# A delta-rule attention block on one core: the order of the q/k/v products, what GpSimd convolves, and where squares and a square root stand

## The reference, cut to what matters

```
q = silu(short_conv(x @ Wq + bq, q_conv)); q = q / (norm(q per head) + 1e-6)
k = silu(short_conv(x @ Wk + bk, k_conv)); k = k / (norm(k per head) + 1e-6)
v = silu(short_conv(x @ Wv + bv, v_conv))
alpha = sigmoid(x @ Wa + ba); beta = sigmoid(x @ Wb + bb)
out_gate = silu(x @ Wg + bg)
```

## Time and profile before

| | us |
|---|---|
| median of 3 runs | 3601.69 |
| lowest, highest | 3601.07, 3607.35 |
| the profiled execution | 3599.55 |
| its span | 3597.8 |

### The profile page before, as it was taken

One profiled execution on the slowest core, in us unless ns is written; L12 is line 12 of the kernel. 1 busy time (PEld: TensorE's weight loads), 2 busy tenths in 40 slices (PEclk: granted clock), 3 DMA queues, 4 the chain that ended last, 5 costly groups with the idle time before them and its releaser, 6 DMA issues. The chain is left out here.

```text
span 3597.8 us, 192259 instructions
## 1 busy us (share of the span) xinstructions
PE 3307.7 (92%) x83216; PEld 2763.9 (77%) x83216; DVE 2783.0 (77%) x4457; ACT 1577.3 (44%) x2330; POOL 1840.8 (51%) x1713
## 2 busy tenths in 40 slices
PE   6999997799999999995999999999996986999999
PEld 4888886576767676775999999999996774888887
DVE  6767675787878787875888888888887866676765
ACT  3545543577777777671111111111113332545454
POOL 2232322556566565554777777777775431323232
PEclk9999999899999999997999999999998997999999
DMA  2222213132323232326676666666664773212121
GB/s 97 90 93 82 105 70 113 53 102 80 97 84 97 84 97 77 93 73 158 187 187 187 187 188 187 187 189 187 188 187 142 224 236 112 105 70 105 70 105 59
DMA packets 485370, 452.79 MB, mean 126 GB/s; under 512 B 55360, under 2 KB 448704, under 8 KB 465600
## 3 DMA queue, kind: packets, MB, share of 16 engines
q1 hardware_dynamic: 483008, 449.56, 41.3%
q10 hardware_dynamic: 2304, 2.49, 0.3%
HBM read 331.33 MB, written 120.60 MB: 126 GB/s over the span
## 5 line engine op out<-in xcount | busy, mean ns | idle before, releaser
L274 POOL TENSOR_TENSOR ffn_out<-ffn_gate,ffn_xres 128x512 f32<-128x512 f32 x128 | 173.3, 1382 | 790.3 <-DVE ffn_gate L235 789.9
L660 DVE SCALAR_TENSOR_TENSOR ain_conv<-ain_padded,ain_taps,ain_conv 128x512 f32<-128x512 f32 x384 | 416.5, 1085 | 13.6
L1320 ACT ACTIVATE rec_yf<-rec_ps_f 128x256 f32<-128x256 f32 x128 | 49.1, 384 | 632.2 <-DVE rec_f_t L1229 632.2
L761 POOL TENSOR_TENSOR ain_conv<-ain_conv,ain_term 128x512 f32<-128x512 f32 x192 | 272.3, 1418 | 16.0
L1101 POOL TENSOR_TENSOR rec_d_norm<-rec_dmat,rec_early 128x512 f32<-128x512 f32 x128 | 162.8, 1272 | 197.1 <-DVE rec_dmat L1179 197.1
L46 PE MATMUL ffn_ring<-ffn_mixrh,ffn_wrh 128*128 128x512 f32 x512 | 214.7, 419 | 20.4 <-DVE ffn_mixrl L180 20.4
L816 ACT ACTIVATE ain_buf<-ain_conv 128x512 f32<-128x512 f32 x192 | 121.0, 630 | 232.6 <-POOL ain_conv L761 147.1
L46 PE MATMUL ffn_ring<-ffn_mixkh,ffn_wkh 128*128 128x512 f32 x512 | 216.4, 423 | 0.0
L1376 PE MATMUL rec_ps_scores<-rec_qk_pe,rec_kb 32*32 32x64 f32 x8192 | 141.9, 217 | 70.3 <-issue 46.0
L46 PE MATMUL ffn_ring<-ffn_mixrh,ffn_wrl 128*128 128x512 f32 x512 | 201.9, 394 | 0.0
L46 PE MATMUL ffn_ring<-ffn_act_h,ffn_wvh 128*128 128x512 f32 x512 | 201.9, 394 | 0.0
(11 more groups left out here) (234 smaller groups left out, 10279.3 us busy)
## 6 DMA issues: line engine op xcount, KB each, us to landing
rec_early<-coeffs SPq DMA_DIRECT2D x512, 128.0 KB, 3.0
streams<-ain_buf SPq DMA_DIRECT2D x48, 1024.0 KB, 5.1
rec_qkv<-streams SPq DMA_DIRECT2D x126, 384.0 KB, 3.3
rec_qk_pe<-streams SPq DMA_DIRECT2D x127, 256.0 KB, 3.1
rec_late<-coeffs SPq DMA_DIRECT2D x504, 64.0 KB, 2.0
ffn_x<-in_x SPq DMA_DIRECT2D x16, 1024.0 KB, 8.4
ffn_xres<-in_x SPq DMA_DIRECT2D x16, 1024.0 KB
x<-ffn_out SPq DMA_DIRECT2D x16, 1024.0 KB, 4.6
```

What stands on the lines that cost most here:

```text
L274: last = nc.gpsimd.tensor_tensor(out[:, m, :], gate[:, m, :], xres[:, m, :], ALU.add)
L660: nc.vector.scalar_tensor_tensor(out=out[:], in0=pad[:, n:n + TOK], scalar=taps[:, u // KT, u % KT, n:n + 1], in1=out[:], op0=ALU.mult, op ...
L761: nc.gpsimd.tensor_tensor(out[:], out[:], term[:], ALU.add).then_inc(pool_conv, 1)
L1320: nc.scalar.activation(yf[:, 1], ps_f[:, :, 1, :], ACT.Copy).then_inc(f2_ready, 1)
```

## The change

The units are dealt out anew: u % 3 = 2 is v (unit 2 is v 0, 5 is v 1, 8 is v 2, 11 is v 3), the others are q 0 to 3 and k 0 to 3 in order. So the products run q q v q q v k k v k k v, and the units on GpSimd, which keep their numbers, are v. The head sums go to units 0, 1, 3, 4, 6, 7, 9, 10 and stand behind products 5, 6, 8, 9, 11, 12, 13 and 14.

`mask_tails` and its mask are gone. In a sequence's first tile (s = 0) the three columns in front are filled with zeros and the tail is saved; in the second (s = 1) the tail is copied in and not saved.

ScalarE runs shift 0 and shift 1 ahead of the squares of the next tile, and the Sqrt of the head sums stands between gates 2 and 3. VectorE convolves unit 0 ahead of the centring. SyncE stores q after 5 silus, k after 11 and v after 12.

```diff
-        D_STEPS, D_UNITS, P_STEPS, P_UNITS = TAPS + 1, 8, 2 * TAPS, 4
+        D_UNITS, P_UNITS = 8, 4
+        D_STEPS, P_STEPS = (TAPS + 1, TAPS), (2 * TAPS, 2 * TAPS - 1)
...
+        def unit(u):
+
+            return (2, u // 3) if u % 3 == 2 else divmod(row(u), KT)
+
+        def row(u):
             return u // 3 * 2 + u % 3
...
-                for j in range(3):
-                    sp.wait_ge(silued, 12 * t + 4 * j + 4)
+                for j, units in ((NQ, 5), (NK_, 11), (NV, 12)):
+                    sp.wait_ge(silued, 12 * t + units)
...
-            nc.vector.memset(start_mask[:], 1.0).then_inc(mask_ready, 1)
...
# VectorE, convolve (GpSimd's has the same two cases)
-                nc.vector.tensor_copy(pad[:, 0:TAPS - 1], tail[:, u, :]).then_inc(conv_step, 1)
-                dve.wait_ge(conv_step, at + 1)
-                nc.vector.tensor_copy(tail[:, u, :], pad[:, TOK:TOK + TAPS - 1]).then_inc(conv_step, 1)
+                if s == 0:
+                    nc.vector.memset(pad[:, 0:TAPS - 1], 0.0).then_inc(conv_step, 1)
+                    dve.wait_ge(conv_step, at + 1)
+                    nc.vector.tensor_copy(tail[:, row(u), :], pad[:, TOK:TOK + TAPS - 1]).then_inc(conv_step, 1)
+                    at += 1
+                else:
+                    nc.vector.tensor_copy(pad[:, 0:TAPS - 1], tail[:, row(u), :]).then_inc(conv_step, 1)
...
# VectorE, slot
-                mask_tails(t)
+                convolve(t, s, 0)
                 if ahead:
                     centre(t + 1)
-                for u in (0, 1, 3, 4):
-                    convolve(t, u)
+                for u in (1, 3, 4):
+                    convolve(t, s, u)
...
# GpSimd, slot
-                pool.wait_ge(tails_masked, t + 1)
...
# ScalarE, silu: a square for q and k alone, in the order of their rows
                 if j < 2:
+                    n = row(u)
                     act.wait_ge(silued, 12 * t + u + 1)
-                    if u >= 4:
-                        act.wait_ge(heads_summed, 8 * t + u - 3)
+                    if n >= 4:
+                        act.wait_ge(heads_summed, 8 * t + n - 3)
...
# ScalarE, slot
-                if more:
-                    act.wait_ge(heads_summed, 8 * t)
-                    square(t + 1)
                 for u in range(12):
-                    shift(t, u)
+                    shift(t, s, u)
+                    if more and u == 1:
+                        act.wait_ge(heads_summed, 8 * t)
+                        square(t + 1)
                     if u > 1:
-                        silu(t, u - 2, more)
+                        silu(t, s, u - 2, more)
...
-                act.wait_ge(heads_summed, 8 * t + 8)
-                nc.scalar.activation(inv_norm[HROWS, :], ps_rows[HROWS, :], ACT.Sqrt).then_inc(rooted, 1)
-                silu(t, 10, more)
+                silu(t, s, 10, more)
...
                 for m in range(KT):
                     if m == 2:
-                        silu(t, 11, more)
+                        silu(t, s, 11, more)
+                    if m == 3:
+                        act.wait_ge(heads_summed, 8 * t + 8)
+                        nc.scalar.activation(inv_norm[HROWS, :], ps_rows[HROWS, :], ACT.Sqrt).then_inc(rooted, 1)
...
# TensorE, slot
+            SUMS_AFTER = {5: 0, 6: 1, 8: 2, 9: 3, 11: 4, 12: 5, 13: 6, 14: 7}
...
-                    j, m = divmod(u, KT)
+                    j, m = unit(u) if u < 12 else (3, u - 12)
...
-                    if 5 <= u < 13:
-                        head_sums(t, u - 5)
+                    if u in SUMS_AFTER:
+                        head_sums(t, SUMS_AFTER[u])
```

More of the change, by code:

```diff
@@ L569, in _ @@
             nc.vector.memset(ones[:], 1.0).then_inc(ready, 1)
[L570 removed]
             nc.vector.memset(head_sum[:], 0.0)
             nc.vector.memset(wab_pad, 0.0)
[L573 to L574 removed]
+            nc.vector.memset(not_first[:], 1.0).then_inc(mask_ready, 1)
             dve.wait_ge(mask_ready, 1)
[L576 to L577 removed]
+            nc.vector.memset(not_first[:, 0:TOK:CH], 0.0).then_inc(mask_ready, 1)
             dve.wait_ge(mask_ready, 2)
@@ L739, in squares, with convolve @@
                 nc.gpsimd.tensor_tensor(sum2[:], half2[:, 0, :], half2[:, 1, :], ALU.add).then_inc(summed2, 1)
-            def convolve(t, u):
-                at = P_STEPS * (P_UNITS * t + u // 3)
+            def convolve(t, s, u):
+                at = before(P_STEPS, P_UNITS, t, s, u // 3)
                 pad, out = padded[2], conv[2]
+                j, m = unit(u)
                 def turn():
@@ L750, in convolve, with slot @@
                 turn()
[L751 to L754, removed]
+                if s == 0:
+                    nc.gpsimd.memset(pad[:, 0:TAPS - 1], 0.0).then_inc(pool_conv, 1)
+                    pool.wait_ge(pool_conv, at + 1)
+                    turn()
+                    nc.gpsimd.tensor_copy(tail[:, D_UNITS + m, :], pad[:, TOK:TOK + TAPS - 1]).then_inc(pool_conv, 1)
+                    at += 1
+                else:
+                    nc.gpsimd.tensor_copy(pad[:, 0:TAPS - 1], tail[:, D_UNITS + m, :]).then_inc(pool_conv, 1)
                 for n in range(TAPS - 1):
+                    pool.wait_ge(pool_conv, at + 1 + 2 * n)
+                    turn()
+                    nc.gpsimd.tensor_scalar(term[:], pad[:, n:n + TOK], taps[:, j, m, n:n + 1], 1.0,
+                                            ALU.mult, ALU.mult).then_inc(pool_conv, 1)
                     pool.wait_ge(pool_conv, at + 2 + 2 * n)
[L757 to L760, removed]
                     nc.gpsimd.tensor_tensor(out[:], out[:], term[:], ALU.add).then_inc(pool_conv, 1)
-            def slot(t, more):
-                pool.wait_ge(tails_masked, t + 1)
+            def slot(t, s, more):
                 if more:
@@ L772, in _ @@
             weight_low("g")
-            with pool.Fori(0, NT - 1) as t:
-                slot(t, True)
-            slot(NT - 1, False)
+            with pool.Fori(0, NT // 2 - 1) as r:
+                slot(2 * r, 0, True)
+                slot(2 * r + 1, 1, True)
+            slot(NT - 2, 0, True)
+            slot(NT - 1, 1, False)
         @block.scalar
@@ L804, in shift, with silu @@
                     act.wait_ge(silued, 12 * t + u - 2)
-                nc.scalar.activation(conv[u % 3][:], ring[u % 4][:], ACT.Identity, bias=bias_tap[:, u:u + 1],
-                                     scale=taps[:, u // KT, u % KT, TAPS - 1:TAPS]).then_inc(biased, 1)
-            def silu(t, u, more):
-                j, m = divmod(u, KT)
-                wait_convolved(act, t, u)
+                nc.scalar.activation(conv[u % 3][:], ring[u % 4][:], ACT.Identity, bias=bias_tap[:, j * KT + m:j * KT + m + 1],
+                                     scale=taps[:, j, m, TAPS - 1:TAPS]).then_inc(biased, 1)
+            def silu(t, s, u, more):
+                j, m = unit(u)
+                wait_convolved(act, t, s, u)
                 if m == 0:
                     act.wait_ge(stored[j], 16 * t)
-                    for n in "qkv"[j * 3:]:
-                        act.wait_ge(w_split[n], 1)
+                    if u == 0:
+                        for n in "qkv":
+                            act.wait_ge(w_split[n], 1)
                 view = buf[:, :, j, m, :]
```

47 lines of the change are left out of this document (21 added, 26 removed).

## The result

The changed kernel takes 3679.06 us (median of 4 runs, 3674.84 to 3684.07) against 3601.38 for the kernel before beside it: ratio 1.0218, 95% interval 1.0206 to 1.023, so 78 us slower. The profiled execution took 3684.07, with a span of 3682.1; the one before took 3599.55. All but 1 us of the difference between the two spans arises in the q/k/v stage: there the last operation ends at 1710.84 in place of 1627.45, 83.4 us later.

The account below looks back on a forecast made before the run. TensorE, busy 868.4 of 918.4 us, was taken as nearly the bound. Slot 0 costs 1.3 us and slots 1 to 15 6.4 each, 97.3 on 3599.55: forecast 3698, range 3655 to 3735.

Parts of the forecast that it names:

- Squares of 2 and 5 gone, gain 1.8: ScalarE's path loses the squares of units 2 and 5 and its wait at unit 2: 1.8 us gained.
- Head sums 6 and 7 ahead of units 14 and 15: TensorE needs unit 10's square ahead of unit 15, so the a/b product starts at 20.1, against 13.9.
- Sqrt behind silu 11: ScalarE's Sqrt ends at 22.3 against 12.3, so VectorE's norms end at 27.9 against 20.4, late by 7.5 us.
- Unit 0 ahead of the centring: VectorE convolves unit 0 from 27.9, so centring ends at 32.9, 10.0 us later; GpSimd's unit 2 from 38.8.
- Zeros: On GpSimd, a fill costs the same as a copy in even slots; odd slots save 0.8 us per unit.
- Reload of the table, stores, setup: ScalarE's table reload at the loop's head is hidden; later stores and the setup's mask fills change nothing.
- GpSimd undisturbed: Rival, chance 0.15: GpSimd's units 2 and 5 take 8.6 us each, 2.5 less a slot, giving 3661.
- The clock falls: Rival, chance 0.13: TensorE's clock falls after waits of about 3 us, 1.5 us lost each, giving 3721 to 3743.
- further drain at a change of table set: Rival, chance 0.02: ScalarE's table switch costs more than its row; another 1.28 us gives 3717, the skill's 1.38 some 21.

Follow-up runs that it names:

- e2: Changed kernel with head sums 6 and 7 moved behind products 14 and 15: 3674.53 us, ratio 1.0198 to the kernel before.
- b2: Kernel before with evictions 0 and 1 ahead of the squares and unit 0's convolution ahead of the centring: 3641.86 us, ratio 1.0117.
- e4: Changed kernel with centring put back ahead of unit 0's convolution and squares ahead of evictions 0 and 1: 3666.96 us, ratio 1.0182.
- b1: Kernel before with zeros in place of the masked tails alone: 3597.84 us, ratio 0.9984.
- m4: e3 with the next tile but one prepared at the end of a slot: 3582.57 us, ratio 0.9948 to the kernel before.
- e3: Changed kernel with the Sqrt behind silu 10 and head sums 6 and 7 behind products 14 and 15: 3645.45 us, ratio 1.0116.
- e5: e3 with centring put back ahead of unit 0's convolution and squares ahead of evictions 0 and 1: 3630.35 us, ratio 1.0070.
- m2: b1 with the next tile but one prepared at the end of a slot, its centring ahead of the norms: 3555.34 us, ratio 0.9871.

## Why the prediction was right

The sign and the mechanism were right, the size a quarter too large: 3698 was forecast and 3679.06 measured, a cost of 97 us against 78. In the terms of the sum: a slot was to take 67.7 and takes 66.3 to 66.7; sixteen slots were to add 97.3 and add 83.4 in the profiled execution (15 x 5.28 = 79.2, the last slot 3.9, the start 0.2).

1. **Squares of 2 and 5 gone, gain 1.8.** Held: from silu 2 to the end of eviction 5 it takes 4.7, from silu 5 to the next zero 6.1 (forecast 4.7 and 6.0).
2. **Head sums 6 and 7 ahead of units 14 and 15.** a/b product at 20.1, measured 19.6. e2 shows that this chain is real and that it hides behind the other one.
3. **Sqrt behind silu 11.** Forecast 22.3, measured 21.5; norms to 27.9, measured 26.6. The step that was mis-sized is step 5, which this one builds on: I took the fill in even tiles for as dear as the copy. It takes 0.10, where the copy took 0.64, and so unit 8 and silu 8 are 0.6 and silu 11 0.8 earlier. The norms take 5.1, not 5.5: their first operation takes 0.42 while GpSimd is idle, 0.81 beside it.
4. **Unit 0 ahead of the centring.** Forecast: centring ends 32.9, unit 2 from 38.8; measured 31.5 and 37.5, the same 1.3 or so as above. b2 shows that this step alone costs 39.6 us, e4 that undoing it alone gives only 12 back: the norms are late anyway, and unit 2 takes longer.
5. **Zeros.** Right for the odd tiles (0.19 for the copy, no save), wrong for the even ones, as said. b1 gives their own worth: 4 us.
6. **Reload of the table, stores, setup.** Nothing shows. The load again starts 1.29 ahead of its Sqrt (986.73, 988.02). The Trainium skill's further drain at a change of table set (ScalarE: Activation LUTs, What ACT_TABLE_LOAD costs) shows here no more than it did in the rows of before.

Of the rivals, *GpSimd undisturbed* (3661) had its share: unit 2 took 8.1, where I had 8.5 for the odd and 9.3 for the even tile. Unit 5 took 9.7 in both, where I had 9.6 for the odd and 10.4 for the even tile. So for an even tile both of its units came out shorter, by 2.0 us, for an odd one only unit 2, by 0.4. *The clock falls* did happen, at about the places named, and cost a few tenths of a us a slot here. After the wait of 2.14 ahead of head sum 6, with the columns of the earlier trace rows:

```profile
978.30:981.70 3.40, 3.40 (x9) 2.31 (x7) 2.87 (x3) 0.42 (x1) 3.11 (x3) 0.50 0.00 0
```

The granted clock is 0.50, the level of 1.2 GHz, and product 14 takes 4.52 us from its first matmul to its last, where product 13 took 2.97. But head sum 7 would otherwise have waited for the square of unit 10, which ended at 982.66; it starts at 983.11 without a wait. Slots of the same trace show the price. The slot from 1498.50 has no fall ahead of its a/b product, though TensorE waits 2.97 and 2.14 there too: the product starts at 19.3 in place of 19.6, and the next zero is at 66.15 in place of 66.3. From an odd tile the clock is mostly low for 6.9 us around zero, and the slot takes 66.7; in the slot from 1166.47 it is low for 3.5 us, and the slot takes 66.3. So 0.15 to 0.4 us a slot at least.

The small price isn't general. It is small here because a wait for the next square follows, which the slower matmuls use up. In m4 no such wait follows, and the rival's price of 1.5 us a fall is reached and passed. Here are two of its slots from an odd tile, with like waits ahead of head sum 4 (first two rows) and the columns of the earlier trace rows (last two):

```profile
876.46 1.13 PE L913 MATMUL ain_ps_rows<-ain_sq,ain_head_sum 128*128 128x512 f32 x2 [2.04 <-ACT ain_sq L838]
...
995.12 1.98 PE L913 MATMUL ain_ps_rows<-ain_sq,ain_head_sum 128*128 128x512 f32 x2 [2.02 <-ACT ain_sq L838]
...
876.41:935.51 59.10, 57.42 (x232) 42.77 (x232) 47.35 (x54) 45.84 (x63) 35.46 (x34) 1.00 0.31 92
995.07:1056.14 61.07, 59.13 (x232) 43.36 (x232) 42.38 (x54) 45.95 (x64) 35.63 (x34) 0.97 0.29 89
```

The slot with the fall takes 2.0 us more, 1.7 of it in TensorE's busy time. In e3 and e5 a fall at zero goes with 0.4 to 0.9 us a slot. This is read from slots of one trace beside each other; no run took the falls away by itself.

That the forecast lay high has two reasons. From an even tile it had 67.8 and the slot takes 66.3: unit 2 starts 1.3 earlier (the fill and the shorter norms, step 3) and takes 0.4 less, and 0.2 are lost again behind it. From an odd tile it had 67.9 and the slot takes 66.7: unit 2 starts 0.7 later than forecast (38.0 and not 37.3), but units 2 and 5 are 2.0 shorter. The second reason shows in other runs too: each engine's times were taken as fixed when work was moved, but GpSimd's units come out shorter when VectorE's move away from them. This gives back part of a delay (b2: 1.2 of 4.6 at unit 2) and takes back part of a gain (e4: 1.3 of 2.8).

## What to carry to other kernels

When a change moves work along hand-ordered queues, follow two things through the slot: what the moved work now stands behind, and what stood behind it. Here the norms came late. Their results delayed nothing (in m2 they end 3.4 us later than in b1, and the slot is shorter); but behind them, and behind unit 0, stood the preparation of the next tile, for which GpSimd waits. Preparing that tile before the norms is worth 42.5 us in the old order and 63 in the changed one, and with the old order and zeros it beats both kernels (3555.34 us). A gain of such a cure isn't the cost of the change: make the same edit in the kernel before too, and compare. Where two chains of like length end at one point, undoing one alone shows next to nothing, so test them together before calling either innocent.

## What the runs showed of the hardware

- The same GpSimd convolution takes from 8.0 to 9.4 us (unit 2, tail not saved) by what VectorE does beside it, and the swing tracks VectorE's own: three multiply-adds take 2.33 alone (994.14) and 2.6 to 4.7 beside GpSimd. The prediction had this as a rival, not in its sum. It isn't told apart here which overlap of the two costs how much.
- A fill of 128 x 3 on GpSimd takes 0.10 in every slot seen; the copy of the same shape takes from 0.19 to 0.96 in the rows shown.
- TensorE's granted clock fell to 0.50, the level of 1.2 GHz, for 3.4 to 3.5 us or twice that at a time, some 20 times in the changed kernel's stage; the kernel before and m2 have no such fall between the stage's first 9 us and its last product. The length of the wait ahead doesn't tell a fall by itself: in m4 it came with a wait of 2.02 and not with one of 2.04, and in the changed kernel the wait of 2.97 in the slot from 1498.50 had none. What a fall costs depends on what TensorE does next: 2.0 us in the slot of m4, 0.15 to 0.4 in the changed kernel, where it runs into the next wait.
